# Output projection of an attention layer in split form, and the decay sums moved one step later

## The chip, the cores and the metric

The kernel runs on one core of a Trainium2 chip. Its time is the device time of one execution in microseconds (us). The engines are PE (TensorE, matmuls; its weight loads are shown as PEld), DVE (VectorE), ACT (ScalarE), POOL (GpSimd) and SP (SyncE, which issues the DMAs). Each engine works through a program of its own, in order, and waits on semaphores for the others.

## What is computed

Input are 4096 tokens of width 256 (2 sequences of 2048). The attention layer works on 16 heads of width 16 with a decay and a weight by the level of distance. In the reference:

```python
Y = jnp.einsum('bhts,bshd->bthd', Wmat, V).reshape(Bb, Tt, H * HD)
o = Y @ Wout.T + x                       # the output projection, then an inner norm
...
x = _layernorm(x + _L0_attn_ref(...), axis=-1)
x = _layernorm(x + _L0_ffn_ref(...), axis=-1)   # a gated recurrence over 2 steps, on all 4096 tokens
```

The decay of a head is `exp(cg[t] - cg[s])`, with `cg` a cumulative sum over the tokens of `g`.

## The kernel before

The tokens are cut into 32 chunks of 128 tokens, and pairs of chunks make 16 groups of 256 tokens (`sg`). All engines run the same loop over steps, `STEPS = range(-3, NG + 13)`, four steps to a chunk; the order in each step is written out by hand. Chunk `ci` has its exponents at step 4ci, its scores at step 4ci+1, its weighted values (`weigh`) at step 4ci+4, and its output projection (`out_proj`) at step 4ci+6. Work on the next group is spread over eight steps: eight projections of queries and keys (`project(sg, j)`, j = 0 to 7, one a step), the token projections (`tokens`), and the decay sums (`decays`, which are four fp32 matmuls on `ng` and the triangle in `cs`). Of these, j = 2 stands at a step that is 1 modulo 8, j = 3 at 2 modulo 8, j = 4 at 3 modulo 8; `decays` stands at 2 modulo 8, between the output projection of an odd chunk and j = 3.

The projections already are in split form: `mm3` takes a high and a low part (fp32r) of both factors and adds three products in one bank, high by high, high by low, low by high. The output projection isn't: it multiplies `yt` (128 tokens by 256, fp32) by `wo` (256 by 256, fp32), in two fp32 matmuls of 128x256, which the profile shows as four records. A split needs a copy to fp32r (on ACT, for the high part) and a subtraction (on DVE or POOL, for the low part).

What a projection waits for matters below. `project` with j = 1, 2, 3 and 5, 6, 7 writes bank 0, and waits (on `a_qk`) until ACT has copied out the result of the one before it in that bank; j = 0 and 4 write another bank and wait for DVE's weighting (`d_w`):

```python
                if not project_bank(j):
                    e.wait_ge(a_qk, 8 * sg + (j - 1 if j % 4 == 1 else j))
```

DVE's order around a chunk's y is, at step 4ci+5: `turn_y(ci)` (from bank `YB`, with the part of earlier chunks in `zs` added, to `yt`), the two multiplications of `weights` of the next chunk, then `inter` of the next chunk; the sum that goes through the norm (`oo`) follows a step later. POOL meanwhile adds x (`x1`), and makes `AT` and `prod` for the exponents (`levels`), one operation behind the other. All matmuls are recorded on L383 (`mm`), the tiled ones on L407 (exponents), L439 (`weigh`), L474 (`inter`) and L503 (`state`), the transposes on L386. DVE's two-operand operations are on L979, POOL's on L1351, ACT's on L751.

At the end the recurrence (`units_at`, from step 127) starts while chunks 30 and 31 are still at their norms; there PE works on 128x512 products `yH,wH`, and the output projection of chunk 31 stands between two groups of them.

Of the kernel before, what the change touches and what calls it, by code (L numbers as in the profile page):

```python
# [5 lines left out]
P = 128  # L6
# [39 lines left out]
def token_jobs(s):  # L46

    out = []
    for d, j in ((12, 7), (0, 0), (0, 1), (1, 2), (3, 8), (5, 3), (7, 4), (8, 5)):
        n = s + 11 - d  # L50
        if n % 8 == 0 and (0 if j == 7 else 1) <= n // 8 < NSG:
            out.append((n // 8, j))
    return out
# [21 lines left out]
def misc_jobs(s):  # L75

    out = []
    if 0 <= s < NG:
        ci, cc = s // 4, (s // 4) % CB
        if s % 4 == 0:  # L80
            out += [("keys", ci, 0), ("keys", ci, 1)]
        if s % 4 == 1 and cc:
            out += [("inter", ci, 0), ("inter", ci, 1)]
        if s % 4 == 3 and cc < CB - 1:
            out += [("state", ci, 0)]
    for sg, j in token_jobs(s):
        if j == 3:
            out += [("cgt", sg, 0)]
        if j == 5:
# [66 lines left out]
def program(nc, x, xT, wqk, wtok, wout, wffn, cst, bcv, fv, out):  # L156
    ctx = ExitStack()
    with ctx:
        scr = nc.dram_tensor("scr", (8, 8, 2, 128), F32, kind="Internal").ap()

        def sb(name, shape, dt=F32):
            return ctx.enter_context(nc.sbuf_tensor(name, shape, dt))

        def sem(name):
            return ctx.enter_context(nc.semaphore(name))
# [7 lines left out]
        xt = [sb(f"xt{i}", [P, 2, 256]) for i in range(2)]  # L173
        wo = sb("wo", [P, 2, 256])
        cs = sb("cs", [P, C_CT])
        bv = sb("bv", [P, B_END])
        fvs = sb("fvs", [P, 8])
        yt = sb("yt", [P, 256])
        oo = sb("oo", [P, 256])
        x1 = sb("x1", [P, 256])  # L180
        st1 = sb("st1", [P, 6])
# [69 lines left out]

        wt0 = W[:, :, :].rearrange("p h t -> p (h t)")[:, 0:928].rearrange("p (k n) -> p k n", k=2)
        w0 = [t[:, :, :].rearrange("p m t -> p (m t)") for t in (QT[1], KT[1])]

# [15 lines left out]
        p_sc, p_x, p_y, p_kt = sem("p_sc"), sem("p_x"), sem("p_y"), sem("p_kt")  # L270
        p_in, p_st, p_op, p_cf = sem("p_in"), sem("p_st"), sem("p_op"), sem("p_cf")
        g_v0, g_s0 = sem("g_v0"), sem("g_s0")
        p_b0, p_turn, p_gate, p_o = sem("p_b0"), sem("p_turn"), sem("p_gate"), sem("p_o")
# [3 lines left out]
        a_dv, a_dec, a_coef = sem("a_dv"), sem("a_dec"), sem("a_coef")  # L277
        a_e = sem("a_e")
        a_wf, a_c0, a_yh, a_g = sem("a_wf"), sem("a_c0"), sem("a_yh"), sem("a_g")
# [5 lines left out]
        d_red, d_ct = sem("d_red"), sem("d_ct")  # L285
        d_w, d_yt, d_S = sem("d_w"), sem("d_yt"), sem("d_S")
        d_oo, d_mv1, d_nn, d_mv2, d_x2 = [sem(n) for n in ("d_oo", "d_mv1", "d_nn", "d_mv2", "d_x2")]
# [17 lines left out]
        def _(e):  # L305
# [37 lines left out]
            e.dma_start(C[:, :, :].rearrange("p h l -> p (h l)"), cst[:, C_CT:C_END]).then_inc(l_c, 16)  # L343
            e.dma_start(wo[:, :, :], kt(wout)).then_inc(l_wo, 16)
            load_x(0)
# [35 lines left out]
        def _(e):  # L381
# [126 lines left out]
            def out_proj(ci):  # L508
                e.wait_ge(d_yt, ci + 1)
                if ci == 0:  # L510
                    e.wait_ge(l_wo, 16)
                for k in range(2):
                    t = mm(YB[:, 256:512], yt[:, 128 * k:128 * k + 128], wo[:, k, :], k == 0, k == 1)
                t.then_inc(p_op, 1)
# [188 lines left out]
            for s in STEPS:  # L703
# [14 lines left out]
                if (c1 := chunk_at(s, 6)) is not None:  # L718
                    out_proj(c1)
                for sg, j in token_jobs(s):  # L720
                    if j == 3:
                        decays(sg)
                for sg, j in project_jobs(s):
                    project(sg, j)
                if n == 3 and ci in STATE:
# [23 lines left out]
        def _(e):  # L749
# [83 lines left out]
            def exps(ci):  # L833
# [105 lines left out]
            for s in STEPS:  # L939
                if 0 <= s < NG and s % 4 == 0:  # L940
                    exps(s // 4)
                if (sg := split_x_at(s)) is not None:
                    split_x(sg)
                if s == NG - 4:
                    act(c0H[:, :, :], bc(c0, 2, 2), ACT.Copy).then_inc(a_c0, 1)
# [28 lines left out]
        def _(e):  # L974
# [76 lines left out]
            def turn_y(ci):  # L1051

                e.wait_ge(p_y, 2 * ci + 2)
                if ci:
# [71 lines left out]
            def outer_stats(ci):  # L1126
                nonlocal made
                e.wait_ge(g_x1, ci + 1)
                e.bn_stats(st2[:, :], x1[:, :]).then_inc(d_own, 1)
                made += 1  # L1130
                e.wait_ge(d_own, made)
                e.bn_aggr(mv2[:, :], st2[:, :]).then_inc(d_mv2, 1)  # L1132

            def outer_norm(ci):
                e.wait_ge(g_rs2, ci + 1)
                e.tensor_scalar(xs[:, ci, :], x1[:, :], mv2[:, 0:1], rs2[:, 0:1], ALU.subtract, ALU.mult).then_inc(d_x2, 1)

# [166 lines left out]
            for s in STEPS:  # L1304
                if (ci := chunk_at(s, 5)) is not None:
                    turn_y(ci)
                if 0 <= s < NG and s % 4 in (1, 2):
                    weights(s // 4, s % 4 - 1)
                for sg, j in token_jobs(s - 1):
                    if j in (5, 7):  # L1310
                        turn_levels(2 * sg + (j - 5) // 2)
# [35 lines left out]
        def _(e):  # L1347
# [103 lines left out]
            decayed_values(0)  # L1451
            for s in STEPS:
                if s == NG - 4:
                    e.wait_ge(a_c0, 1)
                    tt(c0L[:, :, :], bc(c0, 2, 2), c0H[:, :, :], ALU.subtract).then_inc(g_c0, 1)
# [114 lines left out]
```

## Time and profile before

| | us |
|---|---|
| median of 3 runs | 691.07 (690.83 to 691.55) |
| the profiled execution | 691.23 |
| its span | 689.4 |
| PE busy in the span | 667.5 (97%) |
| DVE, POOL, ACT busy | 473.2, 348.2, 339.6 |

The span runs from the first to the last instruction that the profiler recorded, and the execution has 1.8 us outside it. A record of a matmul is longer than its share of PE, since the next one begins before it ends: what a matmul costs is read from the distance of two starts. In the views below, an operation is named by what it writes and reads (`bank<-wo,yt`), and the text in square brackets is how long its engine sat idle before it and what ended that.

### The profile page before, as it was taken

What the parts mean: (1) busy time and instruction counts of PE and PEld (TensorE: products, weight loads), DVE (VectorE), ACT (ScalarE), POOL (GpSimd) and SP (SyncE); (2) the same over time, 40 slices, a digit from 0 to 9 for tenths busy, and PEclk for the clock granted to TensorE, in tenths of its full rate; (3) what the DMA queues carried; (4) which work ended last, traced back from release to release, by engine and by line L of the source; (5) the groups of instructions that cost most, each with busy time, mean ns of one, the idle gap of its engine ahead of it and who ended that gap; (6) DMA issues with size and microseconds to landing.
All of it is one profiled execution on the core that took longest, in us unless ns stands there. A gap on an engine that the chain in (4) does not pass through costs nothing.

```text
span 689.4 us, 22147 instructions
## 1 busy us (share of the span) xinstructions
PE 667.5 (97%) x9194; PEld 604.7 (88%) x9194; DVE 473.2 (69%) x1072; ACT 339.6 (49%) x759; POOL 348.2 (51%) x471
## 2 busy tenths in 40 slices
PE   9799999999999999999999999999978999999994
PEld 7699999999999999899999999999967888888894
DVE  3854877769786868667696868688896435454546
ACT  5545454445545554444455455545433434555555
POOL 2705555646465565656364655655455125343434
PEclk9999999999999999999999999999987899999998
DMA  8112130303131221203031212213032000000002
GB/s 303 40 45 58 41 88 11 98 7 94 30 70 41 60 57 42 68 2 98 8 91 32 68 48 52 69 31 82 3 98 63 1 1 1 31 31 31 31 32 92
DMA packets 53588, 37.09 MB, mean 54 GB/s; under 512 B 5360, under 2 KB 52080, under 8 KB 53488
## 3 DMA queue, kind: packets, MB, share of 16 engines
q1 hardware_dynamic: 53488, 35.67, 19.0%
q8 instruction: 73, 1.20, 0.8%
q14 instruction: 27, 0.22, 0.1%
HBM read 30.41 MB, written 5.24 MB: 52 GB/s over the span
## 4 chain that ended last, share of the span: by engine, by line
PE 90%; DVE 3%; ACT 2%; SPq 1%; DMA 1%; POOL 1%; issue 1%; POOLq 0%; DVEq 0%; ACTq 0%
PE bank L383 66%; PE bank L386 6%; PE bank L407 5%; PE bank L474 5%; PE bank L439 5%; PE bank L503 4%; SPq L330 1%; DMA xt<-in_wffn 1%; DVE t L982 1%; ACT t L751 0%; DVE st L1279 0%; DVE hh L979 0%; DMA scr<-cT 0%; DVE t L979 0%; ACT QT L751 0%
## 5 line engine op out<-in xcount | busy, mean ns | idle before, releaser
L383 PE MATMUL bank<-xH,wH 128*128 128x256 f32 x480 | 144.6, 301 | 0.0
L383 PE MATMUL bank<-xL,wH 128*128 128x256 f32 x480 | 135.0, 281 | 0.0
L383 PE MATMUL bank<-xH,wL 128*128 128x256 f32 x480 | 134.3, 280 | 0.0
L979 DVE TENSOR_TENSOR W<-bank,E 128x512 f32<-128x512 f32 x128 | 82.2, 684 | 34.7 <-PE bank L383 34.7
L383 PEld LDWEIGHTS bank<-xH,wH 128*128 128x128 f32 x480 | 90.5, 189 | 6.3 <-issue 5.5
L383 PEld LDWEIGHTS bank<-xL,wH 128*128 128x128 f32 x480 | 90.7, 189 | 0.4
L383 PEld LDWEIGHTS bank<-xH,wL 128*128 128x128 f32 x480 | 90.5, 188 | 0.0
L751 ACT ACTIVATE E<-bank 128x512 f32<-128x512 f32 x128 | 66.1, 603 | 49.0 <-PE bank L407 49.0
L751 ACT ACTIVATE QT<-bank 128x512 f32<-128x512 f32 x64 | 38.2, 596 | 100.7 <-PE bank L383 100.7
L383 PE MATMUL bank<-QT,KT 64*128 64x128 f32 x1024 | 65.9, 278 | 1.2 <-ACT E L751 1.2
L383 PEld LDWEIGHTS bank<-QT,KT 64*128 64x128 f32 x1024 | 59.7, 188 | 5.6 <-ACT E L751 1.5
L751 ACT ACTIVATE KT<-bank 128x512 f32<-128x512 f32 x64 | 38.0, 594 | 51.7 <-PE bank L383 51.7
L1351 POOL TENSOR_TENSOR lr<-mv,cs 128x1 f32<-128x1 f32 (+1 forms) x80 | 18.3, 228 | 80.8 <-DVE mv L1132 74.9
L1351 POOL TENSOR_TENSOR rs<-lr,cs 128x1 f32<-128x1 f32 (+1 forms) x80 | 51.7, 647 | 6.3
L1351 POOL TENSOR_TENSOR x<-oo,xs 128x256 f32<-128x256 f32 x32 | 23.5, 735 | 60.2 <-DVE oo L982 57.6
L1351 POOL TENSOR_TENSOR t<-t 128x416 f32<-128x416 f32 x42 | 46.6, 1110 | 3.4
L407 PE MATMUL bank<-CT,AT 32*128 32x128 f32 x1024 | 39.1, 291 | 9.3 <-ACT QT L751 5.2
L979 DVE TENSOR_TENSOR g<-g 128x512 f32<-128x512 f32 (+1 forms) x26 | 17.6, 677 | 38.7 <-ACT g L751 38.4
L407 PEld LDWEIGHTS bank<-CT,AT 32*128 32x128 f32 x1024 | 32.9, 193 | 10.6 <-DVE CT L1206 5.3
L1351 POOL TENSOR_TENSOR xL<-xt,xH 128x512 fp32r<-128x512 f32 x15 | 19.1, 1273 | 44.5 <-ACT xH L751 44.5
L751 ACT ACTIVATE t<-t 128x416 f32<-128x416 f32 x64 | 35.3, 552 | 12.6 <-DVE t L1164 7.8
L1351 POOL TENSOR_TENSOR prod<-ll,cs 128x512 f32<-128x512 f32 x32 | 40.7, 1271 | 1.2 <-DVE ll L979 1.2
(151 smaller groups left out, 1686.9 us busy)
## 6 DMA issues: line engine op xcount, KB each, us to landing
cB<-scr SPq DMA_DIRECT2D x240, 64.0 KB, 2.9
xt<-in_xT SPq DMA_DIRECT2D x16, 256.0 KB, 3.0
xs<-in_x SPq DMA_DIRECT2D x16, 256.0 KB, 3.2
out<-xs SPq DMA_DIRECT2D x16, 256.0 KB, 2.1
xt<-in_wffn SPq DMA_DIRECT2D x8, 256.0 KB, 3.1
QT<-in_wqk SPq DMA_DIRECT2D x4, 256.0 KB, 5.8
KT<-in_wqk SPq DMA_DIRECT2D x4, 256.0 KB, 6.1
scr<-cT SPq DMA_DIRECT2D x16, 64.0 KB, 1.9
```

Of the source, the lines that this page charges most:

```text
L330: e.dma_start(cB[c][16 * a:16 * a + 16, :, :, :].rearrange("p l u t -> p (l u) t"), scr[a, :, c, :].partition_broadcast(16)).then_inc(l_cB ...
L383: return e.matmul(o, a, b, start=start, stop=stop)
L386: return e.transpose(o, i, ident)
L407: m = e.matmul(XP[q][:, :].rearrange("p (h t) -> p h t", h=H)[:, :, 8 * j:8 * j + 8], AT[b][r, j, :], CT[b][r, :].rearrange("p (h t) -> p ...
L439: y = e.matmul(YB[32 * n:32 * n + 32, 128 * k:128 * k + 128], V[sg % 3][:, c, v:v + 32], W[:, h, :], start=u == 0 and k == 0, stop=u == 1, ...
L474: t = e.matmul(MB[MISC["inter", ci, k][0]][32 * n:32 * n + 32, 128 * i:128 * i + 128], S[r, l, n, 16 * o:16 * o + 32], QT[b][r, 4 * o + n, ...
L503: t = e.matmul(MB[m][k:k + 64, 16 * q:16 * q + 16], Kt[:, 128 * q + k:128 * q + k + 64], Vw[b][:, c, 128 * h + 16 * q:128 * h + 16 * q + 1 ...
L751: return e.activation(o, i, f, **kw)
L979: return e.tensor_tensor(o, a, b, op)
L982: return e.scalar_tensor_tensor(out=o, in0=a, scalar=s, in1=b, op0=op0, op1=op1)
L1351: return e.tensor_tensor(o, a, b, op)
```

## The change

The output projection takes `mm3` with `ytH`, `ytL`, `woH`, `woL`. `wo` is loaded into the tile `zt`, and split once, at step 1, by ACT and POOL. `yt` goes: `turn_y` adds in place in `zs`, ACT copies that to `ytH` (`split_y`, at the head of step 4ci+5), DVE makes `ytL` after the weights of the same step. The sum with x goes in place to `xs` and `x1` goes. And `decays(sg)` stands a step later (`d` 6 in place of 5, so at 3 modulo 8) and behind that step's projection.

```diff
-    for d, j in ((12, 7), (0, 0), (0, 1), (1, 2), (3, 8), (5, 3), (7, 4), (8, 5)):
+    for d, j in ((12, 7), (0, 0), (0, 1), (1, 2), (3, 8), (6, 3), (7, 4), (8, 5)):
...
             def out_proj(ci):
-                e.wait_ge(d_yt, ci + 1)
+                e.wait_ge(d_yl, ci + 1)
                 if ci == 0:
-                    e.wait_ge(l_wo, 16)
-                for k in range(2):
-                    t = mm(YB[:, 256:512], yt[:, 128 * k:128 * k + 128], wo[:, k, :], k == 0, k == 1)
+                    e.wait_ge(g_wo, 1)
+                for k in range(2):
+                    c = slice(128 * k, 128 * k + 128)
+                    t = mm3(YB[:, 256:512], ytH[:, c], ytL[:, c], woH[:, k, :], woL[:, k, :], k == 0, k == 1)
                 t.then_inc(p_op, 1)
...
                     out_proj(c1)
+                for sg, j in project_jobs(s):
+                    project(sg, j)
                 for sg, j in token_jobs(s):
                     if j == 3:
                         decays(sg)
-                for sg, j in project_jobs(s):
-                    project(sg, j)
...
+            def split_wo():
+                e.wait_ge(l_wo, 16)
+                act(woH[:, :, :], wo0, ACT.Copy).then_inc(a_wo, 1)
+
+            def split_y(ci):
+                e.wait_ge(d_yt, ci + 1)
+                if ci:
+                    e.wait_ge(p_op, ci)
+                act(ytH[:, :], zs[ci % 2][:, :], ACT.Copy).then_inc(a_yt, 1)
...
+                if (ci := chunk_at(s, 5)) is not None:
+                    split_y(ci)
                 if (sg := split_x_at(s)) is not None:
                     split_x(sg)
...
+            def split_y(ci):
+                e.wait_ge(a_yt, ci + 1)
                 if ci:
                     e.wait_ge(p_op, ci)
-                if ci in INTER:
-                    e.wait_ge(d_own, summed[ci])
-                    tt(yt[:, :], YB[:, 0:256], zs[ci % 2][:, :], ALU.add).then_inc(d_yt, 1)
-                else:
-                    e.tensor_copy(yt[:, :], YB[:, 0:256]).then_inc(d_yt, 1)
+                tt(ytL[:, :], zs[ci % 2][:, :], ytH[:, :], ALU.subtract).then_inc(d_yl, 1)
...
-                    tt(x1[:, :], oo[:, :], xs[:, ci, :], ALU.add).then_inc(g_x1, 1)
+                    tt(xs[:, ci, :], oo[:, :], xs[:, ci, :], ALU.add).then_inc(g_x1, 1)
```

On PE, at step 10 (chunk 1's projection of y, group 2's projection j = 3), there stood before:

```order
L383 MATMUL bank<-xH,wL 128x256
L383 MATMUL bank<-wo,yt 128x256 [waits d_yt]
L383 MATMUL bank<-wo,yt 128x256
L383 MATMUL bank<-ng,cs 128x32 [waits m_free0,d_gg]
L383 MATMUL bank<-ng,cs 128x32
L383 MATMUL bank<-cs,ng 128x128 x2
L383 MATMUL bank<-xH,wH 128x256 [waits a_qk,g_xl]
```

At the same place of the changed kernel there stands:

```order
L385 MATMUL bank<-woH,ytH 128x256 [waits d_yl]
L385 MATMUL bank<-woL,ytH 128x256
L385 MATMUL bank<-woH,ytL 128x256
L385 MATMUL bank<-woH,ytH 128x256
L385 MATMUL bank<-woL,ytH 128x256
L385 MATMUL bank<-woH,ytL 128x256
L385 MATMUL bank<-xH,wH 128x256 [waits a_qk,g_xl]
```

Six products stand for two matmuls, and the decay sums no longer stand between j = 2 (whose last product is the first row of before) and j = 3 (the last row of both).

On DVE, in the step before (step 9, turning y of chunk 1), there stood before:

```order
L979 TENSOR_TENSOR yt<-bank,zs 128x256 [waits d_own,p_op,p_y]
L979 TENSOR_TENSOR W<-bank,E 128x512 [waits p_y,a_e,p_sc]
L979 TENSOR_TENSOR W<-bank,E 128x512
L979 TENSOR_TENSOR zs<-bank,cB 128x128 [waits l_cB0,p_in]
L979 TENSOR_TENSOR zs<-bank,cB 128x128
```

And in the changed kernel there stands at this place:

```order
L996 TENSOR_TENSOR zs<-bank,zs 128x256 [waits d_own,p_y]
L996 TENSOR_TENSOR W<-bank,E 128x512 [waits p_y,a_e,p_sc]
L996 TENSOR_TENSOR W<-bank,E 128x512
L996 TENSOR_TENSOR ytL<-zs,ytH 128x256 [waits p_op,a_yt]
L996 TENSOR_TENSOR zs<-bank,cB 128x128 [waits l_cB0,p_in]
```

The subtraction `ytL`, which the output projection waits for, stands behind the two multiplications of the next chunk's weights.

## Rows read from the trace of the kernel before

**Rows 1.** The page: busy time and share of each engine, granted clock in 40 slices
```profile
PE 667.5 (97%) x9194; PEld 604.7 (88%) x9194; DVE 473.2 (69%) x1072; ACT 339.6 (49%) x759; POOL 348.2 (51%) x471
...
PEclk9999999999999999999999999999987899999998
```

**Rows 2.** The page: the chain that ended last, by engine
```profile
PE 90%; DVE 3%; ACT 2%; SPq 1%; DMA 1%; POOL 1%; issue 1%; POOLq 0%; DVEq 0%; ACTq 0%
```

**Rows 3.** Waits of PE in the whole span: us in total, times, longest
```profile
PE bank L407 <- ACT QT L751: 5.2, 2, 4.4
PE bank L407 <- DVE CT L1206: 4.1, 2, 3.8
```

**Rows 4.** Timeline of PE, chunk 17's projection: start us, us, engine, line, operation
```profile
324.26 0.28 PE L383 MATMUL bank<-xL,wH 128*128 128x256 f32 x1
...
325.56 1.03 PE L383 MATMUL bank<-wo,yt 128*128 128x256 f32 x4
326.42 0.53 PE L383 MATMUL bank<-ng,cs 128*128 128x32 f32 x4
...
327.43 0.28 PE L383 MATMUL bank<-xL,wH 128*128 128x256 f32 x1
```

**Rows 5.** Timeline at step 2: PE from the end of j = 2, and ACT
```profile
43.39 0.53 PE L383 MATMUL bank<-ng,cs 128*128 128x32 f32 x4
43.59 0.60 ACT L751 ACTIVATE QT<-bank 128x512 f32<-128x512 f32 x1 [2.57 <-PE bank L383]
...
44.33 0.35 PE L383 MATMUL bank<-xH,wH 128*128 128x256 f32 x1
44.52 0.28 PE L383 MATMUL bank<-xL,wH 128*128 128x256 f32 x1
```

**Rows 6.** Timeline of DVE, POOL and ACT around chunk 17's projection
```profile
323.60 0.42 DVE L979 TENSOR_TENSOR yt<-bank,zs 128x256 f32<-128x256 f32 x1
323.94 1.28 DVE L979 TENSOR_TENSOR W<-bank,E 128x512 f32<-128x512 f32 x2
324.46 1.09 POOL L1351 TENSOR_TENSOR AT<-cs,cgt 128x512 f32<-128x512 f32 x1
325.51 1.26 POOL L1351 TENSOR_TENSOR prod<-ll,cs 128x512 f32<-128x512 f32 x1
325.76 0.60 ACT L751 ACTIVATE QT<-bank 128x512 f32<-128x512 f32 x1 [2.69 <-PE bank L383]
```

**Rows 7.** DVE's sum of two tiles in SBUF (ns min/median/max), and one beside POOL
```profile
L979 DVE TENSOR_TENSOR zs<-zt x22: 424/751/1078, 87.6 to 528.2; 128x256 f32<-128x256 f32 x22
...
339.22 1.27 POOL L1351 TENSOR_TENSOR prod<-ll,cs 128x512 f32<-128x512 f32 x1
339.89 0.88 DVE L979 TENSOR_TENSOR zs<-zt 128x256 f32<-128x256 f32 x1
```

**Rows 8.** Timeline of DVE, POOL and PE, chunk 13's projection
```profile
261.38 1.28 DVE L979 TENSOR_TENSOR W<-bank,E 128x512 f32<-128x512 f32 x2
261.91 1.08 POOL L1351 TENSOR_TENSOR AT<-cs,cgt 128x512 f32<-128x512 f32 x1
263.71 1.03 PE L383 MATMUL bank<-wo,yt 128*128 128x256 f32 x4
```

**Rows 9.** The same of chunk 15's projection: DVE, POOL and PE
```profile
294.11 1.28 DVE L979 TENSOR_TENSOR W<-bank,E 128x512 f32<-128x512 f32 x2
294.64 1.09 POOL L1351 TENSOR_TENSOR AT<-cs,cgt 128x512 f32<-128x512 f32 x1
294.93 1.02 PE L383 MATMUL bank<-wo,yt 128*128 128x256 f32 x4
```

**Rows 10.** Timeline around chunk 31's projection, and ACT's 128x256 fp32r copy
```profile
546.41 1.33 POOL L1351 TENSOR_TENSOR c1L<-c,c1H 128x512 fp32r<-128x512 f32 x1 [13.13 <-ACT c1H L751]
546.50 0.42 DVE L979 TENSOR_TENSOR yt<-bank,zs 128x256 f32<-128x256 f32 x1
547.47 1.02 PE L383 MATMUL bank<-wo,yt 128*128 128x256 f32 x4
...
L751 ACT ACTIVATE c2H<-g 128x256 fp32r<-128x256 f32 x2 | 0.8, 418 | 2.6 <-DVE g L979 2.6
```

More of the change, by code:

```diff
@@ L83, in misc_jobs @@
             out += [("inter", ci, 0), ("inter", ci, 1)]
-        if s % 4 == 3 and cc < CB - 1:
-            out += [("state", ci, 0)]
     for sg, j in token_jobs(s):
@@ L88, in misc_jobs @@
             out += [("cgt", sg, 0)]
+    if 0 <= s < NG and s % 4 == 3 and cc < CB - 1:
+        out += [("state", ci, 0)]
+    for sg, j in token_jobs(s):
         if j == 5:
@@ L173, in program @@
         xt = [sb(f"xt{i}", [P, 2, 256]) for i in range(2)]
-        wo = sb("wo", [P, 2, 256])
+        woH, woL = [sb(n, [P, 2, 256], F32R) for n in ("woH", "woL")]
         cs = sb("cs", [P, C_CT])
@@ L177, in program @@
         fvs = sb("fvs", [P, 8])
-        yt = sb("yt", [P, 256])
+        ytH, ytL = [sb(n, [P, 256], F32R) for n in ("ytH", "ytL")]
         oo = sb("oo", [P, 256])
-        x1 = sb("x1", [P, 256])
         st1 = sb("st1", [P, 6])
@@ L252, in program @@
         wt0 = W[:, :, :].rearrange("p h t -> p (h t)")[:, 0:928].rearrange("p (k n) -> p k n", k=2)
+        wo0 = zt[:, 0:2, :]
         w0 = [t[:, :, :].rearrange("p m t -> p (m t)") for t in (QT[1], KT[1])]
@@ L271, in program @@
         p_in, p_st, p_op, p_cf = sem("p_in"), sem("p_st"), sem("p_op"), sem("p_cf")
+        g_wo = sem("g_wo")
         g_v0, g_s0 = sem("g_v0"), sem("g_s0")
@@ L277, in program @@
         a_dv, a_dec, a_coef = sem("a_dv"), sem("a_dec"), sem("a_coef")
-        a_e = sem("a_e")
+        a_e, a_wo, a_yt = sem("a_e"), sem("a_wo"), sem("a_yt")
         a_wf, a_c0, a_yh, a_g = sem("a_wf"), sem("a_c0"), sem("a_yh"), sem("a_g")
@@ L285, in program @@
         d_red, d_ct = sem("d_red"), sem("d_ct")
-        d_w, d_yt, d_S = sem("d_w"), sem("d_yt"), sem("d_S")
+        d_w, d_yt, d_yl, d_S = sem("d_w"), sem("d_yt"), sem("d_yl"), sem("d_S")
         d_oo, d_mv1, d_nn, d_mv2, d_x2 = [sem(n) for n in ("d_oo", "d_mv1", "d_nn", "d_mv2", "d_x2")]
@@ L343, in _ @@
             e.dma_start(C[:, :, :].rearrange("p h l -> p (h l)"), cst[:, C_CT:C_END]).then_inc(l_c, 16)
-            e.dma_start(wo[:, :, :], kt(wout)).then_inc(l_wo, 16)
+            e.dma_start(wo0, kt(wout)).then_inc(l_wo, 16)
             load_x(0)
@@ L941, in _ @@
                     exps(s // 4)
+                if (ci := chunk_at(s, 5)) is not None:
+                    split_y(ci)
                 if (sg := split_x_at(s)) is not None:
                     split_x(sg)
+                if s == 1:
+                    split_wo()
                 if s == NG - 4:
@@ L1051, in turn_y @@
             def turn_y(ci):
+                z = zs[ci % 2][:, :]
                 e.wait_ge(p_y, 2 * ci + 2)
+                if ci in INTER:
+                    e.wait_ge(d_own, summed[ci])
+                    tt(z, YB[:, 0:256], z, ALU.add).then_inc(d_yt, 1)
+                else:
+                    if ci >= 2:
+                        e.wait_ge(a_yt, ci - 1)
+                    e.tensor_copy(z, YB[:, 0:256]).then_inc(d_yt, 1)
+            def split_y(ci):
+                e.wait_ge(a_yt, ci + 1)
                 if ci:
                     e.wait_ge(p_op, ci)
-                if ci in INTER:
-                    e.wait_ge(d_own, summed[ci])
-                    tt(yt[:, :], YB[:, 0:256], zs[ci % 2][:, :], ALU.add).then_inc(d_yt, 1)
-                else:
-                    e.tensor_copy(yt[:, :], YB[:, 0:256]).then_inc(d_yt, 1)
+                tt(ytL[:, :], zs[ci % 2][:, :], ytH[:, :], ALU.subtract).then_inc(d_yl, 1)
             def state(ci):
@@ L1128, in outer_stats @@
                 e.wait_ge(g_x1, ci + 1)
-                e.bn_stats(st2[:, :], x1[:, :]).then_inc(d_own, 1)
+                e.bn_stats(st2[:, :], xs[:, ci, :]).then_inc(d_own, 1)
                 made += 1
@@ L1135, in outer_norm @@
                 e.wait_ge(g_rs2, ci + 1)
-                e.tensor_scalar(xs[:, ci, :], x1[:, :], mv2[:, 0:1], rs2[:, 0:1], ALU.subtract, ALU.mult).then_inc(d_x2, 1)
+                e.tensor_scalar(xs[:, ci, :], xs[:, ci, :], mv2[:, 0:1], rs2[:, 0:1], ALU.subtract, ALU.mult).then_inc(d_x2, 1)
             def tokens(sg, j):
@@ L1308, in _ @@
                     weights(s // 4, s % 4 - 1)
+                if (ci := chunk_at(s, 5)) is not None:
+                    split_y(ci)
                 for sg, j in token_jobs(s - 1):
@@ L1452, in _ @@
             for s in STEPS:
+                if s == 1:
+                    e.wait_ge(a_wo, 1)
+                    tt(woL[:, :, :], wo0, woH[:, :, :], ALU.subtract).then_inc(g_wo, 1)
                 if s == NG - 4:
```

## The prediction

> **What bounds the kernel now.** I read the page first: PE is busy 97% of the span, the next engine, DVE, 69%, and PE's granted clock is at its upper level (2.4 GHz) in nearly all slices but those of 500 to 550 us [rows 1]. The chain that ended last lies on PE for 90% [rows 2]. The waits of PE are few, and the large ones lie at the start and where the clock is down [rows 3]: from 48 to 499 us PE, but for 0.9 us at chunk 16, goes from product to product, with starts evenly spaced. So a microsecond less on PE's path is a microsecond less of time, and a wait that is put before one of its instructions is a loss in full, however short, because there is no idle time to take it up. The question for each edit is therefore whether what PE waits for comes before PE does. For that I read the timeline of all engines around the output projections.
>
> **What the products cost.** Eleven fp32r products of 128x256 take from 324.26 to 325.56 us, 0.118 us each. The four records of the output projection take from 325.56 to 326.42, 0.86 us [rows 4]. Six products make 0.71 us, so each output projection gives 0.15 us back. Of the 32, those of chunks 29 and 30 lie in the stretch of lower clock, where DMAs and ACT set the pace, which leaves 30: **-4.6 us**. Bounds: 0 if nothing came free, -4.9 with all 32.
>
> By the Trainium skill ("FP8 and Floating Point Precision", section "TensorE Precision Notes") a true fp32 product is four passes through the array, high and low by high and low; three products instead of four would then give back a quarter of 0.86, 0.21 us each and 6.5 us in all. The trace disagrees in the size: a product costs 0.118 us, over a quarter of 0.43. I go by the rows.
>
> **What the decays hid.** They take from 326.42 to 327.31 (327.43 less 0.12), 0.89 us, and stand between j = 2 and j = 3 of the projections [rows 4]. j = 3 writes the bank of j = 2, and waits until ACT has copied it. What that wait costs when too little stands between is in the trace, once, at step 2, where no output projection stands yet: j = 2 ends its slot at 43.39, ACT copies from 43.59 to 44.19, and j = 3 starts at 44.33, 0.14 us after the copy and 0.94 us after the slot; its second product comes 0.19 us later in place of 0.12, so the restart costs 0.07 more [rows 5]. ACT's copy stands at the same distance at chunk 17: 325.76 to 326.36, against the slot's end at 325.56 [rows 6]. So 1.01 us must stand between j = 2 and j = 3. Before there was 0.86 + 0.89 = 1.75 us; now there is 0.71. The rest, **0.30 us, is a wait of PE** at each of the 14 steps with both (chunks 1, 3, ... 27), 4.2 us by itself. At step 2 nothing is left as cover, and the decays' 0.89 us come on top of the wait: **+0.9 us**, once. Behind j = 4 the decays are neither hidden nor hiding: PE does them anyway, and DVE's copy of them (behind the state's) is due only at the next step's transposes.
>
> **Whether y's low part is there in time.** Before, PE waited for `yt`, which at chunk 17 ended at 324.02, 1.54 us ahead of the projection. Now it waits for `ytL`: ACT's copy (0.42 us [rows 10]) fits beside the weights, but the subtraction stands behind them, which end at 325.22 [rows 6]. It would begin at about 325.14 (DVE's next operation starts 0.08 before the end of one, as `W` does behind `yt`) and end at 325.56 with the 0.42 us of an undisturbed one. But it reads two tiles in SBUF, and such an operation doesn't run beside POOL's: the sum `zs<-zt` takes 0.42 us alone and 0.75 in the median, and the one at 339.89 ends at 340.77, 0.28 after POOL's `prod` (340.49) [rows 7]. At 325.14 POOL is at `AT`, to 325.55, so `ytL` ends at 325.83. With 0.14 for the semaphore and 0.07 for the restart, as above, PE's slot starts at 326.04. PE wants it at 325.41, since the output projection before it, of the even chunk, gave back 0.15 us, while DVE and POOL hang on the token projections ahead of that one: 0.63 us late. This replaces the wait for ACT, which then is over when the six products are done. Six of the 14 chunks stand so (1, 3, 7, 17, 19, 23; `AT` ends 0.01 before to 0.10 us after the old start of the projection): 6 x 0.63 = **3.8 us**. In seven (5, 9, 11, 13, 21, 25, 27) DVE is further ahead: at chunk 13 `AT` ends at 262.99, `ytL` at 263.27, 0.44 ahead of the old start [rows 8], so only ACT's 0.30 counts: 7 x 0.30 = **2.1 us**. At chunk 15, where the second sequence starts, DVE is late: `AT` ends at 295.73, `ytL` at 296.01, 1.08 after the old start, and with 0.36 as above PE loses **1.4 us** [rows 9]. At the even chunks the projection comes some 5 us after `ytL`, and nothing is lost.
>
> The rule of the Trainium skill ("SBUF — State Buffer", section "SBUF: two separate sides") is that VectorE with two SBUF inputs and GpSimd take a shared pair of ports in turns, each for a whole instruction. By it the subtraction starts when `AT` ends, and the trace agrees (0.28 us after POOL's end).
>
> **Chunk 31.** Its projection stands among the recurrence's products. `yt` ends at 546.92, `ytH` would at about 547.4, POOL is at `c1L` until 547.74, so `ytL` ends at 548.02 and PE starts at 548.23 with the restart, where it now does at 547.47 [rows 10]: **+0.8 us**. Without POOL's part it is 0.6. ACT's gates of that step come about 0.9 us later too, which the wait of PE nearly covers.
>
> **Free edits.** `wo` in `zt` is split at step 1, where ACT and POOL have idle time and the first user is five steps off; in place in `xs` costs what `x1` did. Cover gone, the split would be 0.6 us of ACT and 1.3 of POOL, once. DVE gets 32 subtractions, 0.34 to 0.7 us each, some 16 us more on 473: at the exponents, where it comes closest to PE, this falls ahead of the wait for the tokens and not behind it.
>
> **The sum** against the profiled execution: 691.23 - 4.6 + 0.9 + 3.8 + 2.1 + 1.4 + 0.8 = 695.6 us. The median of the runs is 0.16 lower, so I say **695.5 us**. The case's own range is 693.5 to 697.5 (the lower end without POOL's hold, where the six cost 0.3 less each, chunks 15 and 31 together 0.6 less).
>
> **Rivals.**
> - *It pays in full (10%).* ACT copies and y come before PE after all, as they would if the bank of j = 2 weren't asked for so early or the starts that I read were not the true ones. Against: the same wait stands in the trace at step 2 [rows 5]. Then 691.07 - 4.6 = 686.5, faster.
> - *Only ACT's copy counts (15%).* DVE, which has nothing to wait for but y, runs its subtraction earlier or faster than the rows let me think, and all 14 steps cost 0.30, chunk 31 0.3: 691.07 - 4.6 + 0.9 + 4.2 + 0.3 = 691.9, no difference. For: 0.1 to 0.6 us decide it, on an extrapolated slot.
> - *POOL's next operation goes first (5%).* If `prod` follows `AT` without DVE between, `ytL` at chunk 17 ends at 326.77 + 0.28 = 327.05 and PE loses 1.85 us in place of 0.63 [rows 6]. At 14 chunks that is about 1.2 us more each, 17 us, 712 us in all.
> - *DVE becomes the bound (15%).* It then adds 0.1 to 0.3 us at some of the 31 exponents, which wait for its transposed `CT`; at the ends of the loop they do so already [rows 3]. 1 to 3 us over the forecast, 696.5 to 698.5.
> - The forecast: 55%.
>
> What a measurement tells from no change is about 0.2%, 1.4 us. Above 692.5 lie the forecast, the last two rivals (75%); within it lies the second with little of its neighbours (14%); the first is faster, with a little besides (11%). The range 691.4 to 698.5 takes the forecast, most of the second rival and the fourth, and leaves out the first and third.
>
> **What would show it.** In the changed kernel's trace: six products of 0.118 us at each output projection; j = 3 starting 0.94 us after the end of j = 2 at chunks such as 13, 0.14 us behind ACT's `QT`; at step 2 the same, with nothing between; PE waiting for `ytL` at chunks 1, 3, 7, 15, 17, 19, 23 and 31; `ytL` ending 0.28 us after `AT`; no wait at even chunks. The prediction is wrong if j = 3 follows the six products directly, if `ytL` ends before the slot at chunk 17, or if PE waits at the exponents in the middle of the loop.

## The result, and the profile of the changed kernel

The changed kernel takes 697.41 us (median of 4 runs, 695.40 to 698.26) where the kernel before takes 691.01: ratio 1.0087, 95% interval 1.0063 to 1.0111, so it is slower by 0.6 to 1.1%. The forecast was 695.5 us and slower. Its profiled execution took 696.79 us (span 695.0), 5.56 us more than that of before (691.23).

The page of the changed kernel, as in [rows 1]: PE's busy time is the same to 0.3 us although each projection is shorter, and DVE is busy for 18.5 us more (the forecast said some 16).

```profile
PE 667.2 (96%) x9258; PEld 605.3 (87%) x9258; DVE 491.7 (71%) x1104; ACT 351.4 (51%) x792; POOL 354.5 (51%) x472
...
PEclk9999999999999999999999999999997899999997
```

The waits of PE in the whole span (us in total, times, longest), to be held against [rows 3]:

```profile
PE bank L409 <- DVE CT L1230: 5.2, 3, 4.1
PE bank L385 <- DVE ytL L996: 3.9, 8, 1.1
PE bank L409 <- ACT QT L754: 3.5, 1, 3.5
PE bank L476 <- issue: 2.0, 1, 2.0
```

Three things are new: eight waits for `ytL`, one stand of 2.0 us behind nothing that the profile knows ("issue"), and a first wait for ACT's `QT` that is 0.9 us shorter.

Chunk 17's projection, PE and then DVE, POOL and ACT beside it (start us, us, engine, line, operation), to be held against [rows 4, 6]:

```profile
326.15 0.28 PE L385 MATMUL bank<-xH,wL 128*128 128x256 f32 x1
326.77 0.39 PE L385 MATMUL bank<-woH,ytH 128*128 128x256 f32 x1 [0.34 <-DVE ytL L996]
327.00 0.27 PE L385 MATMUL bank<-woL,ytH 128*128 128x256 f32 x1
...
327.47 0.29 PE L385 MATMUL bank<-woH,ytL 128*128 128x256 f32 x1
327.60 0.28 PE L385 MATMUL bank<-xH,wH 128*128 128x256 f32 x1
...
324.82 1.28 DVE L996 TENSOR_TENSOR W<-bank,E 128x512 f32<-128x512 f32 x2
326.01 0.71 DVE L996 TENSOR_TENSOR ytL<-zs,ytH 128x256 fp32r<-128x256 f32 x1
...
325.34 1.10 POOL L1377 TENSOR_TENSOR AT<-cs,cgt 128x512 f32<-128x512 f32 x1
...
326.47 0.60 ACT L754 ACTIVATE QT<-bank 128x512 f32<-128x512 f32 x1 [1.11 <-PE bank L385]
```

POOL's `AT` ends at 326.44, `ytL` 0.28 us later at 326.72, and PE, whose slot was over at 326.27, starts 0.05 behind `ytL` and restarts slowly (0.23 us for the first product in place of 0.12). The next projection, j = 3, follows the six products at once, because ACT's copy, which it needs, ended at 327.07.

Chunk 13 is the other kind, to be held against [rows 8]: the six products follow without a gap, and now it is j = 3 that starts late, at 264.28 in place of 264.05, 0.15 us behind the end of ACT's copy (264.13).

```profile
263.21 0.29 PE L385 MATMUL bank<-xH,wL 128*128 128x256 f32 x1
263.33 0.28 PE L385 MATMUL bank<-woH,ytH 128*128 128x256 f32 x1
...
263.93 0.28 PE L385 MATMUL bank<-woH,ytL 128*128 128x256 f32 x1
264.28 0.36 PE L385 MATMUL bank<-xH,wH 128*128 128x256 f32 x1
...
262.33 0.70 DVE L996 TENSOR_TENSOR ytL<-zs,ytH 128x256 fp32r<-128x256 f32 x1
...
263.53 0.60 ACT L754 ACTIVATE QT<-bank 128x512 f32<-128x512 f32 x1 [1.86 <-PE bank L385]
```

Chunk 15, against [rows 9]: PE's slot ends at 294.55 and the projection starts 1.27 us later.

```profile
294.43 0.28 PE L385 MATMUL bank<-xH,wL 128*128 128x256 f32 x1
295.82 0.39 PE L385 MATMUL bank<-woH,ytH 128*128 128x256 f32 x1 [1.11 <-DVE ytL L996]
...
295.06 0.70 DVE L996 TENSOR_TENSOR ytL<-zs,ytH 128x256 fp32r<-128x256 f32 x1
```

Step 2, against [rows 5]: j = 2 ends its slot at 41.15, ACT's copy at 41.95, and j = 3 starts at 42.09. That is 0.94 us after the slot and 0.14 behind the copy, the numbers of before, but now with nothing between.

```profile
41.03 0.28 PE L385 MATMUL bank<-xH,wL 128*128 128x256 f32 x1
42.09 0.36 PE L385 MATMUL bank<-xH,wH 128*128 128x256 f32 x1 [0.78 <-ACT QT L754]
...
41.35 0.60 ACT L754 ACTIVATE QT<-bank 128x512 f32<-128x512 f32 x1 [1.55 <-PE bank L385]
```

**Where the 5.56 us lie.** I followed the start of each chunk's output projection through both traces; the difference (after less before) is then a running account:

```
chunk          0      28     29     30     31     last matmul
before us    59.78  499.03 509.47 525.93 547.47  679.62
after us     58.46  500.89 511.45 529.43 553.11  685.20
difference   -1.32  +1.86  +1.99  +3.50  +5.63   +5.59
```

Chunks 1 to 28 cost 3.18 us, which is the forecast's loop (28 products at -0.155 and waits of 3.8 + 2.1 + 1.4 give +2.96). The forecast had +0.9 ahead of chunk 0, where -1.32 stands, and +0.5 behind chunk 28 (two products and the wait of chunk 31), where +3.7 stands. The two misses, -2.2 and +3.2 us, cancel for the most part.

Ahead of chunk 0 the +0.9 is there (step 2). Against it stand 0.9 us less of idle time ahead of the exponents of chunk 0 (they start 3.75 us after the product ahead of them, in place of 4.67) and 1.6 us of clock: behind that idle time, from 34 to 40 us, PE's granted clock is 1.00 in this execution and 0.72 in the profiled one of before. The loop was understood; the start and the tail are what the experiments are for.

The tail in the changed kernel, as the chain in order of time (start us, us, what):

```profile
523.99 1.08 PE bank L385 x18
525.07 2.00 PE bank L476 x125
527.08 2.02 issue
529.10 0.40 PE bank L476 x2
```

Before the last of the 128 small matmuls of `inter(31)` (all but two have a record ahead of it), with no wait of the program near, PE stands for 2 us. Its matmuls before and behind are the same row of code. The DMA records show a queue of 16 KB blocks, 74 of them for the 9258 matmuls and as many weight loads of PE, which I read as PE's program; one of these blocks starts at 526.70, just ahead of the stand. Before, the same 128 matmuls ran in 1.95 us. Behind the stand, the 36 products of `first_bias`, from 530.25 on, took 7.0 us, all but the first six at half clock (0.21 us each); before, 4.9 us, mostly at 0.11.

### The profile page after: what moved, and what is told of

The parts are those of the page before. It is cut to its first block and busy times, and to the rows that moved or that the text cites. A ratio compares the mean times of both kernels' runs of the same rounds, so it can differ in the third digit from the quotient of the medians.

```text
span 695.0 us, 22404 instructions
## 1 busy us (share of the span) xinstructions
PE 667.2 (96%) x9258; PEld 605.3 (87%) x9258; DVE 491.7 (71%) x1104; ACT 351.4 (51%) x792; POOL 354.5 (51%) x472
## 5 line engine op out<-in xcount | busy, mean ns | idle before, releaser
L385 PE MATMUL bank<-xH,wH 128*128 128x256 f32 x480 | 140.9, 294 | 0.8 <-ACT QT L754 0.8
L1377 POOL TENSOR_TENSOR xs<-oo,xs 128x256 f32<-128x256 f32 x32 | 23.8, 743 | 68.9 <-DVE oo L999 68.9
L1377 POOL TENSOR_TENSOR prod<-ll,cs 128x512 f32<-128x512 f32 x32 | 45.9, 1433 | 1.2 <-DVE ll L996 1.2
L385 PE MATMUL bank<-yH,wH 128*128 128x512 f32 (+1 forms) x102 | 39.9, 391 | 0.0
```

What stands on the lines that cost most here:

```text
L385: return e.matmul(o, a, b, start=start, stop=stop)
L1377: return e.tensor_tensor(o, a, b, op)
```

## The experiments

With each group of experiments the kernel before ran on the same chip; its medians were 690.85, 690.88, 691.20 and 691.32 us. A trace is always that of one execution.

**The changed kernel again** (`after_again`), no edit.

> The changed kernel once more, to see how much of its last part repeats. Its four runs so far lie between 695.4 and 698.3 us, a wider spread than that of the kernel before (690.8 to 691.6). In its profile PE stands still from 527.1 to 529.1 us inside the matmuls of inter(31) with nothing in the profile that it waits for, and the matmuls of the first bias behind it run at half the clock. Theory A: that pause comes from PE's instructions being fetched late at this place of the program, and belongs to the kernel: it stands at the same instructions again, and the median is 696 to 698 us. Theory B: it is chance: the pause is not there or elsewhere, and the runs fall in two groups some 2 to 4 us apart.

Measured: 699.53 us (696.45 to 699.99, 5 runs), ratio 1.0121 (1.0101 to 1.0140). The median lies above the 696 to 698 us of theory A, but the stand in `inter(31)` is there again (1.6 us), ahead of the same matmul, the last but one. The executions of this kernel spread over 3.5 us. The trace shows one reason: the exponent matmuls of chunk 0 start at 34.16 where the first trace has 34.09, and behind the same idle time PE's granted clock is 0.66 in one and 1.00 in the other (stretch, its length, busy times, PEclk, DMA). First the first trace, then this one:

```profile
30.00:40.00 10.00, 6.53 (x93) 5.98 (x92) 6.92 (x15) 7.39 (x17) 1.27 (x3) 1.00 0.42 107
```
```profile
30.00:40.00 10.00, 6.53 (x58) 6.13 (x57) 5.82 (x13) 5.96 (x14) 1.21 (x3) 0.66 0.42 107
```

Chunk 0's projection comes at 58.46 in one and at 60.94 in the other, with the same instructions: 2.5 us that say nothing of the change. From chunk 0 to 28 this trace loses 3.06 us on before, as the first with 3.18.

**The split alone, decays in their old step and place** (`split_only`):

```
-    for d, j in (... (3, 8), (6, 3), (7, 4), ...):
+    for d, j in (... (3, 8), (5, 3), (7, 4), ...):
...
+                for sg, j in token_jobs(s):
+                    if j == 3:
+                        decays(sg)
                 for sg, j in project_jobs(s):
                     project(sg, j)
```

> The split of y and wo alone, the decays back at their old step and ahead of j = 3. My theory (the decays hid ACT's copy): step 2 gives 0.9 us back, and the 14 odd chunks lose only what y's low part is late, 5.5 us in place of 7.3, so the time is 2.7 us below the changed kernel, 694.5 to 695 us if the end stays as it is. The rival (the move of the decays is harmless, all of the loss is y's low part): no difference to the changed kernel, 697 us.

Measured: 695.71 us (692.77 to 698.16, 6 runs), ratio 1.0074 (1.0049 to 1.0099). From chunk 0 to 28 it lost 2.42 us, not the 0.8 that the forecast's own terms give once ACT's copy is covered again (-4.4 + 3.8 + 1.4). The time between PE's last product and the projection, less the 0.12 of a product, gives the wait for `ytL` at each odd chunk, and it is the same to 0.03 us in this kernel and in the changed one: 0.56, 0.50, 0.60, 0.50, 0.51, 0.60 at chunks 1, 3, 7, 17, 19, 23; 1.27 at 15; 0 at 13; but 0.07 at 5 and 21, and 0.19 to 0.22 at 9, 11, 25 and 27. So in six of the seven chunks that I had put down as free of it, `ytL` is late as well. In the changed kernel that doesn't show in the time, since PE would stand for ACT's copy there anyway. So the decays' move costs 0.6 to 0.8 us of the loop and not the 1.8 that I expected; the 0.9 at step 2 are given back as expected. The medians (1.7 us below the changed kernel's first, 3.8 below its second) can't tell these terms apart.

**The decays alone, the projection still fp32** (`decays_only`), the other half of the diff on the kernel before.

> The kernel before with only the decays moved. My theory: between j = 2 and j = 3 there stands the fp32 output projection alone, 0.86 us of the 1.01 that ACT's copy needs, so 0.15 us are lost at 14 steps, and 0.9 us at step 2: 3.0 us slower, 694 us. The rival (moving the decays is harmless): 691.0 us.

Measured: 694.15 us (694.06 to 694.64, 5 runs), ratio 1.0053 (1.0037 to 1.0069). The trace loses 0.15 to 0.18 us at each of the 14 steps with an odd chunk's projection, and nothing elsewhere in the loop: the four fp32 records take 0.86 us, ACT's copy wants 1.01 between j = 2 and j = 3, and PE starts j = 3 at 0.94 and restarts slowly.

```profile
328.98 1.03 PE L384 MATMUL bank<-wo,yt 128*128 128x256 f32 x4
329.92 0.36 PE L384 MATMUL bank<-xH,wH 128*128 128x256 f32 x1
```

Step 2 lost its 0.9 too. This confirms that the decays were cover, and of which length. That the median also comes out (694 expected) is in part luck: besides its 0.9 the start lost 1.2 us (later by 0.8 before any of the edit is reached, and 0.4 of clock), and the tail gave 1.5 back.

**The split without the decays' move, `ytL` on GpSimd** (`split_pool`): POOL subtracts ahead of `AT` at odd chunks; DVE still does chunk 31's.

```
 # GpSimd
+                yl = chunk_at(s, 5)
+                if yl is not None and yl < NC - 1 and yl % 2:
+                    split_y(yl)
                 for sg, j in token_jobs(s):
...
                     if j in (5, 7):
                         levels(sg, (j - 5) // 2)
+                if yl is not None and yl < NC - 1 and yl % 2 == 0:
+                    split_y(yl)
```

> The split with the decays back and y's low part made by POOL, ahead of AT at odd chunks and behind prod at even ones (DVE still makes that of chunk 31). My theory (y's low part is late because it stands behind the weights on DVE and behind AT at the ports): POOL can begin as soon as ACT's copy is done, at chunk 17 about 0.5 us after y's sum, and takes some 0.75 us, so it is done as PE wants it; what is left are chunk 15 (0.85 us), chunk 31 (0.75), the products' gain (4.6) and the gain at the start that the changed kernel shows (2.2): 685.8 us, and up to 4 more if the end is as in the changed kernel. If y's low part isn't what costs at the odd chunks, the time is that of the split alone, 694 us or more.

Measured: 690.14 us (689.61 to 692.08, 12 runs), ratio 0.9997 (0.9986 to 1.0007). In the loop it does what the products promise: a pair of an even chunk and the odd one behind it gives 0.12 to 0.31 us, but for 14 and 15 (+0.54: PE waits 0.73 us for `ytL` at chunk 15). Chunk 17:

```profile
325.59 0.28 PE L384 MATMUL bank<-xH,wL 128*128 128x256 f32 x1
325.71 0.34 PE L384 MATMUL bank<-woH,ytH 128*128 128x256 f32 x1
...
324.86 0.74 POOL L1381 TENSOR_TENSOR ytL<-zs,ytH 128x256 fp32r<-128x256 f32 x1
325.56 1.09 POOL L1381 TENSOR_TENSOR AT<-cs,cgt 128x512 f32<-128x512 f32 x1
```

From chunk 0 to 28 it gains 2.56 us where the changed kernel loses 3.18. That is the test of the main reason: where `ytL` comes before PE does and the decays cover ACT, the same products are a gain. The whole is not faster, and its median lies above the expectation (685.8 to 689.8). The trace is of the slowest of the 12 executions (692.08). In it three things take the gain away: the stand in `inter(31)` (1.9 us), here as in all split kernels so far; the start, 1.5 us behind before at chunk 0, with a granted clock of 0.53 from 34 to 40 us; and the waits for `ytL` at chunks 29 and 31 (0.5 and 0.7 us).

**What makes PE stand in `inter(31)`** (`before_pad`, `split_pool_pad`, `after_pad`): 128 waits on a count long reached, 64 in each of PE's two long idle times. They compute nothing and move every later instruction of PE's program.

```
 def exponents(ci):
+    for _ in range({0: 64, NC - 1: 64}.get(ci, 0)):
+        e.wait_ge(d_lp, 1)
     e.wait_ge(d_ct, ci + 1)
```

> The kernel before with 128 extra instructions on TensorE's queue that do nothing (waits on a count that is long reached): 64 ahead of the exponent matmuls of chunk 0, where TensorE idles 4.7 us anyway, and 64 ahead of those of chunk 31, where it idles 4.0 us. Every kernel with the split product that ran so far stands still for 1.9 to 2.3 us in the middle of the 128 small matmuls of inter(31), behind no wait, and has about 124 more instructions on TensorE by then than before; the kernels with the fp32 product don't stand still. Theory (the position of the instructions in the blocks in which TensorE's program is fetched decides): the pause of about 2 us appears here too, with no split product in the kernel, and the 16 first_bias matmuls behind it run at half clock earlier: 691 + 2 to 4 = 693 to 695. Rival (the split product itself or its operands cause the pause): no pause, 691.

> The split product with ytL on GpSimd and the decays in their old place, and the same 128 idle instructions on TensorE. Theory (position in the fetched blocks): some 250 instructions more than the kernel before is close to one whole block of 256 (16 KB), so the pause of 1.9 us in inter(31) is gone and part of the half clock behind it: 690.1 - 2 to 4 = 686 to 688, faster than the kernel before by 0.4 to 0.7%. Rival (the pause belongs to the split product): 690, unchanged.

> The changed kernel as it is, with the same 128 idle instructions. Theory: the pause of 2.0 us near 527 us and the earlier half clock behind it (about 1.5 us) are gone, the losses in the loop stay: 697.4 to 699.5 less 2 to 4 = 694 to 697. Rival: unchanged at 697.4 to 699.5.

Measured: `before_pad` 691.96 us (689.27 to 695.12, 11 runs), ratio 1.0020 (1.0007 to 1.0033), and no stand, against the theory; the waits cost 0.4 us ahead of chunk 31's exponents. `split_pool_pad` 690.28 (685.76 to 692.09, 12 runs), ratio 0.9979 (0.9960 to 0.9999); `after_pad` 696.10 (692.46 to 699.20, 7 runs), 1.0072 (1.0046 to 1.0099). In both split kernels the stand is gone: the 128 matmuls of `inter(31)` take 2.47 and 2.07 us in place of 3.92 and 4.36. The row "issue" is no longer among the waits of `split_pool_pad` in the tail (505 to 560 us):

```profile
PE bank L410 <- DVE CT L1235: 4.3, 1, 4.3
PE bank L384 <- POOL ytL L1383: 0.8, 2, 0.4
```

So the data and the semaphores of the split don't by themselves stop PE there. What does is open. The place of the instructions in the fetched blocks is one reading, and the timing speaks for a fetch: in all four traces with a stand (two of the changed kernel, `split_only`, `split_pool`) it lies ahead of the same matmul, and ends 1.3 to 1.5 us after a block of PE's program that began to move 2.4 to 2.9 us before. But the fp32 kernel got no stand from the same shift, and half of the waits stand in the idle time just ahead of chunk 31's exponents, so they also change when PE asks for its program; the runs don't separate the two. `after_pad` lies in its expected range, but its runs and those of the changed kernel overlap. Nor did the medians fall by the full 2 us, and `split_pool_pad` missed its 686 to 688: three of its runs lie at 685.8 to 685.9 (granted clock of the whole 0.984 to 0.985), two at 688.5 to 688.7 and seven at 689.9 to 692.1 (0.975 to 0.982). Its trace is of one of the fastest three, and whether the slower ones stood isn't known.

**The stand in the fp32 kernel** (`before_small`). A block holds about 125 matmuls with their weight loads (9194 in 73 blocks). By chunk 31's exponents the split kernels are 60 matmul records, about half a block, further on than before: 30 projections of six records in place of four. 32 small fp32 matmuls at the start, two records each, give the fp32 kernel 64.

```
+    if ci == 0:
+        e.wait_ge(a_qk, 8)
+        for _ in range(32):
+            e.matmul(YB[:, 0:64], cs[0:32, 0:128], cs[0:32, 0:64], start=True, stop=True, tile_position=(0, 0))
```

> The kernel before with 32 small fp32 matmuls (64 records, each with its weight load) into a free bank in TensorE's 4.7 us of idle time ahead of the exponents of chunk 0; their results are used by nothing. Read against the matmul that runs when a block of TensorE's program is fetched, the split kernels stand 64 matmul records (half a block) further on than the kernel before in the tail, and the 128 waits moved both kinds by about 32. Theory (the place of inter(31) in the blocks decides): these 64 records bring the fp32 kernel to the very place of the split kernels, so it now stands still for 2 us inside the 128 small matmuls of inter(31) near 526 us: about +2, or more where the half clock behind it comes earlier; the kernel 692.5 to 695 (less up to 2 where the small matmuls keep the clock up at 34 to 38 us). Rival (the split kernels stand there because of what the split product does): no pause there, 689 to 691.

Measured: 700.78 us (697.19 to 704.13, 4 runs), ratio 1.0160 (1.0128 to 1.0191), and the expectation failed: the 128 matmuls take 2.22 us, no stand. The time comes from elsewhere. The small matmuls take 0.135 us a record, 8.5 us for an idle time of 4.7, so all of the loop is 4.8 us late, and at chunk 31 ACT's `E` stands behind a `wH` that waits for a DMA, 2.6 us in place of 1.2. The test was spoiled by both: `QT,KT` ran at half clock there (3.4 us in place of 1.9), so PE came to its instructions more slowly. What exactly sets the stand stays open.

**The start** (`pool_late`): the kernel before, with one wait more on GpSimd.

```
 def levels(sg, c):
     ci = 2 * sg + c
+    if ci == 1:
+        e.wait_ge(a_e, 4)
```

> The kernel before, with GpSimd's levels of chunk 1 held at the start until the exponentials of chunk 0 are done, as the split kernels hold it there by their wait for woH. Theory: VectorE's operation t<-pre, which took 1.52 us beside GpSimd's levels, takes 0.59, the exponent matmuls of chunk 0 start 0.9 us earlier, and the kernel takes 690.0 to 690.3 instead of 691; where TensorE's clock also stays at its upper level between 34 and 38 us, up to 2 us less. Rival (the start of the split kernels came from something else in them): no change, 691.

Measured: 690.06 us (688.00 to 691.31, 12 runs), ratio 0.9988 (0.9977 to 0.9999). DVE's `t<-pre`, which took 1.52 us beside POOL's `AT` and `prod` in the kernel before, takes 0.59, and the exponents start 5.06 us after the start of the last projection ahead of them in place of 5.96:

```profile
30.82 0.64 DVE L979 TENSOR_TENSOR pre<-bank,bv 128x208 f32<-128x208 f32 x2
31.49 0.59 DVE L982 SCALAR_TENSOR_TENSOR t<-pre 128x416 f32<-128x416 f32 x1
```

In the split kernels the wait for `woH` at step 1 holds POOL in the same way by accident, and gives the same 0.9 us (the exponents of chunk 0 come 3.75 to 3.77 us after the product ahead of them, in place of 4.67).

**PE kept busy in its two idle times** (`before_warm`, `split_warm`, `after_warm`): unused fp32 matmuls of 256 columns, 7 to 9 ahead of chunk 0's exponents and 8 ahead of chunk 31's, on the kernel before, on `split_pool`, and on the changed kernel.

```
+    if ci:
+        e.wait_ge(d_w, 4 * ci)
+    if ci in (0, NC - 1):
+        e.wait_ge(a_qk, 8 * NSG if ci else 8)
+        for _ in range(8 if ci else 7):
+            mm((XP[1] if ci else YB)[:, 0:256], cs[:, 0:128], cs[:, 0:256])
     e.wait_ge(d_ct, ci + 1)
```

> The kernel before with 9 fp32 matmuls of 256 columns (0.43 us each, 3.9 us) in TensorE's idle time of 4.7 us ahead of the exponents of chunk 0, and 8 (3.4 us) in that of 4.0 us ahead of those of chunk 31; their results are used by nothing. Theory: TensorE's granted clock stays at its upper level behind both stretches, so the matmuls at 34.7 to 39 us run in 3.5 instead of 5 us and those at 515.4 to 519.3 us in 2.1 instead of 3.9 us; the end of the idle times, set by VectorE and ScalarE, doesn't move: 691 - 2 to 4 = 687 to 689. Rival (the fall of the clock is not from this idleness, or it comes back later all the same, as in the stretch from 531 us, where TensorE is busy and the clock is at its lower level): 690.5 to 691.5.

> The split product with ytL on GpSimd and the decays in their old place, and 7 and 8 such matmuls of 256 columns in the same two idle times. They stand for 30 matmul records, as the 128 waits did, so the pause in inter(31) should be gone too. Theory: products -4.5 by 0.15 each, chunks 15, 29 and 31 +2.0 by their waits for ytL, pause gone, clock kept up: 691 - 4.5 + 2.0 - 0.9 (start) - 2 to 4 = 684 to 686, faster than both kernels. Rival (the clock's loss comes back later): 688 to 690.

> The changed kernel, every product, wait and place as it is, with the 7 and 8 unused matmuls in TensorE's two idle times as in split_warm. It takes out of the comparison what differs from execution to execution at the start (clock at 34 to 38 us) and in the tail (the pause in inter(31), the clock around it), and leaves the loop. Theory (the loop's terms of the prediction hold): the changed kernel's chunks 1 to 28 cost +3.2 us on the kernel before where split_pool's gain 2.4, which is 5.6 apart; step 2 without its decays 0.9 more; split_pool's own wait at chunk 29 (0.6) isn't there. 687.6 + 5.6 + 0.9 - 0.6 = 693.5, so 693 to 694.5; against before with the same matmuls (689.4) slower by 4. Rival (most of the loss that was measured, 6.4 to 8.7 us, came from the start and the tail): 690 to 691.

Measured: `before_warm` 689.42 us (688.10 to 691.52, 12 runs), ratio 0.9980 (0.9968 to 0.9993); `split_warm` 687.57 (685.99 to 688.80, 6 runs), 0.9951 (0.9933 to 0.9969), the fastest here and faster than both kernels; `after_warm` 694.17 (692.86 to 694.82, 6 runs), 1.0041 (1.0026 to 1.0055). The gains are smaller than expected (before_warm 1.8 us for 2 to 4, split_warm 687.6 for 684 to 686). The chunk 0 part works in all three (clock 1.00 from 30 to 40 us). At chunk 31 the fillers came 2.5 to 2.9 us into the idle time; in `split_warm` and `after_warm` the clock had already fallen, and they took 6.5 and 6.2 us in place of 3.4, which delayed what they were to help (stretch of `split_warm`, its length, busy times, PEclk, DMA):

```profile
507.00:511.00 4.00, 1.33 (x34) 1.17 (x33) 3.83 (x10) 0.00 (x0) 2.02 (x4) 0.85 0.36 94
511.00:517.40 6.40, 6.40 (x20) 4.88 (x20) 4.29 (x10) 1.26 (x2) 3.24 (x4) 0.56 0.38 118
```

With the fillers no kernel has the stand (`inter(31)` takes 1.95 to 1.96 us), the clock at the start is the same, and the changed kernel's runs spread over 2.0 us in place of 3.5. So the start is out of the comparison: the changed kernel is 4.8 us slower than before with the same fillers (694.17 less 689.42; two chips, on which the kernel before took 691.32 and 691.20), and 6.6 slower than `split_warm`, against 5.9 expected. The traces of `after_warm` and `before_warm` are 3.8 us apart: -0.24 at chunk 0, +2.96 from chunk 0 to 28, where the forecast's terms give the same, and +1.1 behind it. That last part isn't clean: the fillers at chunk 31 took 3.65 us in `before_warm` and 6.2 in `after_warm`.

## Why the prediction was right, and where it was not

- **What bounds the kernel.** Right. In the loop PE's path took every wait in full, those for `ytL` and those for ACT.
- **What the products cost.** Right: six take 0.70 to 0.71 us (263.33 to 264.05), and `split_pool` gains 0.30 to 0.31 at five pairs of projections, 4 and 5 for one, where nothing is waited for. The Trainium skill ("FP8 and Floating Point Precision", section "TensorE Precision Notes") counts four passes for a true fp32 product; by that it would be 0.21 for each projection, if each of my products cost as much as one of the passes. The rows have 0.118 us for the one and 0.108 (0.43 in four) for the other, so they don't bear out the 0.21; they say nothing against the four passes.
- **What the decays hid.** Right, to 0.01 us at step 2 (0.94 behind the slot, 0.14 behind the copy), and `decays_only` shows the same with 0.15 per step, since 0.86 of the 1.01 were still covered. Behind j = 4 the decays cost nothing more: in `decays_only` the loop loses only at the odd chunks.
- **Whether y's low part is there in time.** The six (1, 3, 7, 17, 19, 23): forecast 0.63 each less the product's 0.31 for the pair, 1.9 us in sum; measured 2.1. Chunk 15: forecast 1.09 for the pair, measured 1.09. PE follows `ytL` by 0.05 us and loses 0.10 in its first product, 0.15 in all, where I had 0.14 and 0.07. `ytL` ends 0.28 us after `AT` at all 14 odd chunks of the loop, as forecast; by the Trainium skill ("SBUF — State Buffer", section "SBUF: two separate sides") it takes the shared ports when GpSimd gives them back, and the trace agrees (0.70 us long in place of 0.42, and POOL's `prod` behind it 1.45 in place of 1.26). The seven (5, 9, 11, 13, 21, 25, 27): the sum (0.30 each) was right and one step in it not, which is luck. I had `ytL` 0.44 us ahead at all seven from the row of chunk 13, and it is so only there; at the other six it is 0.07 to 0.21 late. The wait for ACT hid the error. Had the decays stayed, as in `split_only`, the loop would have cost 1.6 us more than my terms say.
- **Chunk 31.** Forecast 0.8 with the restart; measured 0.61 (the gap ahead of the projection is 0.84 in place of 0.23) and 0.10 for the restart. `ytL` took 0.62 us and ended 0.28 behind POOL's `c1L`, as forecast.
- **Free edits.** Wrong in sign: the split of `wo` at step 1 isn't free but a gain of 0.9 us at the start, because it keeps POOL from DVE's `t<-pre` (`pool_late`).
- **The sum.** That it came so near is in part luck. It stopped at the terms of the edit, and missed the start by -2.2 us (0.9 from POOL held back, the rest mostly the clock of that execution) and the tail by +3.2. In the tail it lacked 2.4 us in `inter(31)`, 2.0 of them the stand, and the half clock behind it (2.1 us more in the `first_bias` products); some 1.6 us were regained, 1.0 ahead of the stand and 0.6 behind. The stand is of the size of the loss that was forecast. The median of 697.4 lies 0.1 us inside the upper end of the case's own range (693.5 to 697.5), and that of the same kernel run again, 699.5, outside the wider one. That the clock at the start makes this difference is shown for the two traced executions alone (2.5 us), and argued for the medians. The lower end of the case's own range doesn't come out of its terms either: 695.5 less six times 0.3 and less 0.6 is 693.1.
- **The rivals.** That it pays in full, and that only ACT's copy counts: both are refuted by the eight waits for `ytL`. POOL's next operation did not go first: its record begins at 326.39, but it is stretched, and `ytL` ends at 326.72 and not behind it. DVE did not become the bound in the loop: from 60 to 500 us the only wait at the exponents is that of chunk 16, 0.8 us, as long as before (there put down to ACT's `QT`, here to DVE's `CT`).

That the kernel is slower was right, and in the loop for the stated reasons. Of the 5.6 us between the two traces, 3.2 are the loop's, 3.7 the tail's, of which I had seen 0.5, and -1.3 the start's.

## What to carry to other kernels

Where PE waits for nothing, ask of each faster product whether its operands come sooner too, and what the removed time had covered: here 0.15 us per projection were bought with a subtraction on an engine that was 0.6 us late and with an ACT copy that had 0.30 us too little over it. With the decays back in their place the loss in the loop was 2.4 us, and with the subtraction also on the engine that was free it became a gain of 2.6. Read every case of a pattern, not one for all: six of seven odd chunks were unlike the one that I had read. And before a difference of 2 us is put down to an edit, compare the start and the tail of two executions of the same kernel.

## What the runs showed of the hardware

- PE can stand for 1.6 to 2.0 us with no wait of the program, in a stretch of 128 small matmuls (15 ns each with their weight loads), ending 1.3 to 1.5 us after a 16 KB block of its own program has moved. All four traces of split kernels without unused instructions (three kernels) have it, and none of the four traces of split kernels with them (128 waits, or 15 unused matmuls; half or more of them in the idle time just ahead). What sets it stays open.
- The same idle time of 3.75 us, in the same kernel, is followed by a granted clock of 1.00 in one execution and of 0.66 over the stretch from 30 to 40 us (part of it at 1.2 GHz) in another: 2.5 us from nothing in the program. Of the seven traces with 3.75 to 3.77 us of idle time there, two kept the clock at 1.00 from 34 to 40 us (`after`, `split_only`), and five had 0.50 to 0.72.
- Fillers that start 2.5 us or more into an idle time can meet the lower clock themselves: 8 matmuls took 3.65 us in `before_warm`, 6.5 in `split_warm` and 6.2 in `after_warm`.
- What one turn at the ports costs DVE depends on where it falls. `t<-pre` takes 0.59 us alone and 1.52 in the kernel before, where it begins with POOL's `AT` (30.85 and 30.84), ends 0.45 us after it (32.37 and 31.92), and the `prod` behind takes 1.59 us in place of 1.27.
